# Four depthwise filters in one TensorE step: from 128x32 tiles, one filter at a time, to sixteen 32x32 tiles

## The reference, cut to what matters

```python
def _causal_dw_conv(x_bcl, w_ck):          # one filter for each channel, no sum over channels
    K = w_ck.shape[-1]
    return lax.conv_general_dilated(x_bcl, w_ck[:, None, :], window_strides=(1,),
                                    padding=[(K - 1, 0)], feature_group_count=x_bcl.shape[1])
```

## Time and profile before

| what | us |
|---|---|
| median of three runs (1008.17, 1003.43, 1007.61) | 1007.61 |
| span of the profiled execution | 1004.1 |
| TensorE busy | 932.3 (93%) |
| VectorE busy | 742.6 (74%) |
| ScalarE busy | 650.3 (65%) |
| GpSimd busy | 334.5 (33%) |

### The profile page before, as it was taken

The page is one execution under the profiler, slowest core; times in us unless marked ns, Lnnn a source line. Parts: engine busy times, 40 slices in busy tenths (PEclk is TensorE's granted clock), DMA queues, the critical chain, the costliest instruction groups (busy, mean ns, idle before and its releaser), DMA issues.

```text
span 1004.1 us, 22014 instructions
## 1 busy us (share of the span) xinstructions
PE 932.3 (93%) x7958; PEld 593.9 (59%) x7958; DVE 742.6 (74%) x2882; ACT 650.3 (65%) x1474; POOL 334.5 (33%) x720
## 2 busy tenths in 40 slices
...
GB/s 308 175 2 1 1 1 52 2 83 14 95 128 75 43 70 17 44 22 12 1 12 1 11 11 1 53 60 94 90 97 76 57 21 22 2 11 1 12 1 32
DMA packets 77692, 45.44 MB, mean 45 GB/s; under 512 B 53008, under 2 KB 68880, under 8 KB 77328
## 3 DMA queue, kind: packets, MB, share of 16 engines
...
## 4 chain that ended last, share of the span: by engine, by line
PE 57%; DVE 27%; ACT 8%; POOL 4%; issue 3%; DMA 0%; SPq 0%; POOLq 0%; ACTq 0%; DVEq 0%
PE psum L1101 7%; DVE pool L1588 5%; DVE sol_t L1593 5%; PE psum L558 5%; PE psum L1091 4%; PE psum L859 4%; PE psum L833 3%; PE psum L831 3%; PE psum L994 3%; DVE pool L1531 3%; PE psum L920 3%; PE psum L1085 2%; PE psum L1087 2%; ACT pool L1823 2%; PE psum L567 2%
## 5 line engine op out<-in xcount | busy, mean ns | idle before, releaser
L1809 ACT ACTIVATE pool<-psum 128x512 f32<-128x512 f32 x144 | 84.0, 595 | 64.4 <-PE psum L558 22.4
L2185 POOL TENSOR_SCALAR small<-small 128x4 f32<-128x4 f32 x88 | 22.2, 252 | 283.6 <-DVE small L1173 281.4
L1823 ACT ACTIVATE pool<-pool,small 128x128 f32<-128x128 f32 x224 | 91.5, 486 | 27.3 <-POOL small L2190 27.1
L558 PE MATMUL psum<-sb_const,pool 128*128 128x128 f32 x672 | 100.9, 283 | 6.4 <-ACT pool L1823 2.9
L920 PE MATMUL psum<-pool,firw 128*32 128x512 f32 (+7 forms) x960 | 103.2, 571 | 0.0
L558 PEld LDWEIGHTS psum<-sb_const,pool 128*128 128x128 f32 x672 | 79.3, 145 | 37.9 <-issue 22.3
L2188 POOL TENSOR_TENSOR small<-small,minus_half 128x4 f32<-128x4 f32 x88 | 92.2, 1048 | 7.3
L994 PE MATMUL psum<-pool,sb_l1a 128*128 128x512 f32 x192 | 88.6, 612 | 0.0
L1101 PEld LDWEIGHTS psum<-sb_l1f,pool 128*128 128x128 f32 x640 | 77.2, 192 | 11.3 <-issue 9.5
L1101 PE MATMUL psum<-sb_l1f,pool 128*128 128x128 f32 x640 | 82.8, 278 | 0.0
L1404 DVE TENSOR_TENSOR pool<-pool,psum 128x512 f32<-128x512 f32 x80 | 52.4, 682 | 37.8 <-ACT pool L2095 16.2
...
## 6 DMA issues: line engine op xcount, KB each, us to landing
...
```

The lines of the kernel that those rows point to most:

```text
L558: m = e.transpose(f.ap[:, part(b)], src[:, part(b)], ident)
L1809: e.activation(slot(g, i), f.ap, ACT.Copy).then_inc(f.emptied, 1)
L1823: m = e.activation(dst[:, part(b)], src[:, part(b)], ACT.Identity, bias=v["nm"][:, b:b + 1], scale=v["r"][:, b:b + 1])
```

## The change

- `vsh` is laid out otherwise: row `4u + s` of a block of 32 rows holds channel `u` (of eight) shifted by `s`. `b_sh` writes `v` with four DMAs in place of one and reads it back into every fourth row.
- `b_fir` is one step. For each of eight tap groups it issues sixteen matmuls of 32 rows and 32 columns: the 32 rows are eight channels by four shifts, the 32 columns are these eight channels for each of four filters. Four PSUM banks are filled at once. It stands where `b_fir.3` stood, and `b_fir.0` to `b_fir.2` are gone from the list.
- `b_ez` goes from GpSimd to VectorE, as one bitwise-and with a mask, and stands right before `b_fir` in the list.
- A new setup step `s_w` (16 matmuls and seven VectorE operations) brings the taps to their rows, and `s_b2` makes `firw` by a memset and 16 small products.
- The rows of `router_W1` are loaded in the new channel order (18 DMAs in place of one), and `b_lt`, `b_w`, `b_mx`, `b_ac` take the results in the new layout.

```diff
-c_ft/6 f_gl/2 b_q/1 b_vs/1 f_lg/3 c_fa/6 c_hF/7 b_fir.3/0 b_kk/0
+c_ft/6 f_gl/2 b_q/1 b_vs/1 f_lg/3 c_fa/6 c_hF/7 b_ez/0 b_fir/0 b_kk/0
...
-b_gg/1 b_ks/2 b_k2/2 b_fir.3/1 b_sh/2 b_x.38-40/0 f_e.2/3 b_ez/2 b_x.41-42/0 b_kk/1
+b_gg/1 b_ks/2 b_k2/2 b_ez/1 b_fir/1 b_sh/2 b_x.38-40/0 f_e.2/3 b_x.41-42/0 b_kk/1
...
+b_x.23-24/1 b_ez/2 b_fir/2 b_x.25/1 b_u.0/0 b_x.26-28/1 b_kk/2
+b_gg/3 b_x.32-34/2 b_ez/3 b_fir/3 b_kk/3
+b_gg/4 f_gw/7 b_q/5 b_k/5 g_out/2 b_q/6 b_ez/4 b_fir/4 f_e.0/7 b_kk/4
+b_x.42-44/4 b_q2/6 f_na/7 b_ez/5 b_fir/5 b_kk/5
+b_x.8-20/5 b_ez/6 b_fir/6 b_rs/4 b_xt/4 b_x.21/5 b_rl/4 b_u.0/4 b_x.22/5 b_sh/7 b_kk/6
+b_x.18-31/6 b_ez/7 b_fir/7 b_xt/5 b_p.2/4 b_x.32/6 b_kk/7
...
         def b_sh(g, k):                                    # SyncE
-            e.dma_start(kept, slot(g, 5)).then_inc(sem(f"v_out{a}"), 16)
+            for r in range(4):
+                e.dma_start(by_row[r], slot(g, 5)[32 * r:32 * r + 32]).then_inc(sem(f"v_out{a}"), 16)
...
-                e.dma_start(vsh[32 * s:32 * s + 32, :, s:],
-                            kept.rearrange("(c p) m -> p c m", c=4)[:, :, 0:GT - s]).then_inc(sem(f"shifted{a}"), 16)
+                e.dma_start(vsh[s:P:4, :, s:],
+                            kept.rearrange("(u c) m -> u c m", c=4)[:, :, 0:GT - s]).then_inc(sem(f"shifted{a}"), 16)
...
         def b_fir(g, k):                                   # TensorE
-            o.wait_ge(sem("edge_zeroed"), 3 * g + 3)
+            o.wait_ge(sem("edge_zeroed"), g + 1)
+            heads_f = [begin("b_fir", g, f"h{r}") for r in range(4)]
-            for n, kg in enumerate(kgs):
-                for c in range(4):
-                    col = FIR_GROUPS.index((k, kg)) * 4 + c
-                    m = e.matmul(b4(f.ap)[32 * c:32 * c + 32, :, 4 * kg:], firw[:, col, :],
-                                 vsh[:, c, :, 0:P - 4 * kg], start=n == 0, stop=n == len(kgs) - 1)
+            for kg in range(NKG):
+                for r in range(4):
+                    r_ = slice(32 * r, 32 * r + 32)
+                    for c in range(4):
+                        m = e.matmul(b4(heads_f[r].ap)[32 * c:32 * c + 32, :, 4 * kg:], firw[r_, kg, c, :],
+                                     vsh[r_, c, :, 0:P - 4 * kg], start=kg == 0, stop=kg == NKG - 1)
+                    if kg == NKG - 1:
+                        m.then_inc(heads_f[r].filled, 1)
...
+        def b_ez(g, k):                                    # VectorE
+            cells = slot(g, 8, 4).bitcast(mybir.dt.int32).rearrange("p (q t) -> p q t", t=P)[:, :, 0:3]
+            o.wait_ge(sem(f"shifted{g % NA}"), 64 * (g // NA + 1))
+            o.settle()
+            e.tensor_tensor(cells, cells, edge[:, :].unsqueeze(1).to_broadcast([P, NP, 3]), ALU.bitwise_and).then_inc(
+                sem("edge_zeroed"), 1)
...
         def b_fir(g, k):                                   # ScalarE
-            evacuate("b_fir", g, 3 + k, k)
+            for r in range(4):
+                f = full("b_fir", g, f"h{r}")
+                e.activation(slot(g, 3 + r), f.ap, ACT.Copy).then_inc(f.emptied, 1)
...
         def b_w(g, k):                                     # VectorE
-            e.tensor_tensor(w3, w3, rep(mq, 5), ALU.mult).then_inc(*o.link())
+            e.tensor_tensor(flat(v["spread"]).rearrange("p (q c f) -> p q c f", c=4, f=4), w3[:, :, 0:4].unsqueeze(2).to_broadcast(shp),
+                            mq.unsqueeze(2).unsqueeze(3).to_broadcast(shp), ALU.mult).then_inc(*o.link())
+            e.tensor_tensor(v["ms"], mq, w3[:, :, 4], ALU.mult).then_inc(*o.link())
...
-        def b_ez(g, k):                                    # GpSimd
-            for s in range(1, 4):
-                settle()
-                e.memset(vsh[32 * s:32 * s + 32, :, :, 0:s], 0.0).then_inc(*mark("edge_zeroed", 3 * g + s))
```

More of the change, by code:

```diff
@@ L51 @@
[L51 to L85, removed]
@@ L101 @@
-f_e.4-5/7 b_qs/5 b_q2/5 b_v/6 f_d.0-2/7 b_vs/6 f_d.3/7 b_ks/6 f_d.4/7 b_ez/5 f_d.5/7 f_out/7 b_x.0-3/4 b_ss/5
-b_fir.0/5 b_x.4-5/4 b_k2/6 b_qs/6 b_x.6-7/4 b_sh/6 b_ez/6 b_qn/5 b_x.8-9/4 g_na/3 g_out/3 b_x.10-31/4 b_gg/5
-b_x.32-41/4 b_vT/5 b_x.42-44/4 b_fir.1/5 b_q2/6 f_na/7 b_fir.2-3/5 b_kk/5 b_fir.0/6 b_x.45-52/4 b_ag/5 b_x.53-58/4
-b_vT/6 b_x.59/4 b_ss/6 b_x.60-61/4 b_xo/4 b_tr/7 b_q/7 b_k/7 b_qs/7 b_v/7 b_vs/7 b_sol/5 b_x.0-1/5 b_qn/6 b_x.2-3/5
-b_gg/6 b_x.4-6/5 b_ks/7 b_k2/7 b_fir.1/6 b_x.7/5 b_fir.2/6 b_x.8-20/5 b_fir.3/6 b_rs/4 b_xt/4 b_x.21/5 b_rl/4 b_u.0/4
@@ new lines @@
+f_hid.1/3 f_e.2-3/2 f_hid.2/3 b_sh/1 c_ft/7 f_e.4-5/2 b_qs/1 b_ag/0 b_sol/0 b_x.0-4/0 b_ks/1 b_x.5-6/0 c_nb/6 f_d.0-1/2
+b_x.7/0 f_d.2-4/2 b_q2/1 f_mu/3 b_k2/1 f_d.5/2 b_ss/1 b_x.8/0 f_out/2 b_x.9/0 f_cnt/3 b_x.10/0 c_fa/7 f_gl/3 b_vT/1
+b_x.11/0 b_x.12-13/0 b_qn/1 b_x.14-18/0 f_hid.3-4/3 f_na/2 b_x.19-30/0 f_gw/3 b_tr/2 b_v/2 b_x.31/0 c_park/6 b_x.32-35/0
+f_hid.5/3 b_x.36-37/0 b_k/2 b_vs/2 f_e.0-1/3 b_gg/1 b_ks/2 b_k2/2 b_ez/1 b_fir/1 b_sh/2 b_x.38-40/0 f_e.2/3 b_x.41-42/0
+b_kk/1 b_ag/1 f_d.0-1/3 f_e.3-4/3 c_nb/7 f_e.5/3 b_x.43-46/0 b_q/2 b_x.47/0 b_qs/2 b_q2/2 b_x.48-49/0 f_d.2-4/3
```

253 lines of the change are left out of this document (168 added, 85 removed).

## The result

The changed kernel takes 1103.4 us (median of four runs, 1099.2 to 1105.2) against 1005.5 for the kernel before (median of four, 1001.1 to 1008.2): a ratio of 1.097, 95% interval 1.093 to 1.101. The profiled execution has a span of 1101.7 us (before 1004.1) and a mean granted TensorE clock of 0.909 (before 0.959). Forecast were 1080 and 1037 to 1118: the direction and the mechanism are right, and the size is 23 us short.

The account below looks back on a forecast made before the run. VectorE was taken as the bound in the two filter stages. 51.2 (wait) + 22.4 (clock) + 2.6 (ScalarE) + 2.6 (setup) + 1.5 (`b_w`) - 6.7 - 1.0 = 72.6 us more, forecast 1080 us, range 1037 to 1118.

Parts of the forecast that it names:

- The wait that comes in: At `b_fir` in all eight groups: TensorE waits for `b_ez`, then VectorE stops for the filter step; 51.2 us in sum.
- TensorE's lead there: Group 6: TensorE read as starting the filters at 717.55, 15 us before VectorE reaches that place.
- both engines are 6.1 us earlier here for the waves that went: Group 4: removed waves were in the chain, so the new wait costs only 0.7 us there.
- the 1.0 for group 0: Group 0: a gain of 1.0 us for the piece like group 4's removed waves.
- The tile step: Each sixteen-tile `b_fir` step: taken to last 6.26 us like `b_fir.3`, upper end 7.9 by weight loads.
- rival 3: Filter steps: sixteen tiles don't overlap fully; 7.9 us a step gives 1093, other cases 1105 or 1130; chance 15%.
- The clock: Eight filter steps: TensorE runs at a lower clock after idling, 2.8 us each, 22.4 us in all.
- VectorE's own waits: In the two stages with filters: VectorE's existing waits of 6.7 us give way, subtracted in full.
- The setup: At the start: VectorE's added operations in `s_w` and `s_b2` cost 2.6 us, between 0 and 5.7.
- ScalarE's bunch: Behind the filters in groups 0 and 4: four bunched copies make TensorE wait 1.3 us each, 2.6 in all.
- The second: Behind the filter steps: other engines use the pause and the clock stays up; 1040 us, chance 13%.
- the first: Whole kernel: TensorE was the bound and gets its time back; 1004.6, or 959 if all busy time counted; chance 4%.

Follow-up runs that it names:

- experiment 1: Changed kernel with the eight `b_ez` words 5 to 17 us earlier in the list, so the mask precedes TensorE's need: 1021.5 us, ratio 1.018.
- experiment 2: Kernel before, plus an unused VectorE addition right before each group's `b_fir.3`, which waits for it: 1080.3 us, ratio 1.076.
- Experiment 8: Kernel before with `b_fir.0` to `b_fir.2` cut to four matmuls of 32x8 columns each, `b_fir.3` whole: 1009.7 us, ratio 1.005.
- 3: Kernel of experiment 1 with the two inner loops of `b_fir` swapped, so neighbouring matmuls lie in different row blocks: 1025.5 us, ratio 1.022.
- 4: Changed kernel with unread matmuls of 128x384 columns filling TensorE's idle time before each `b_fir` wait: 1090.6 us, ratio 1.085.
- 5: Kernel of experiment 1 with `b_fir`'s matmuls over two of the four sequences, half the token columns: 1024.0 us in one run.
- 6: Kernel of experiment 1 with `b_fir` loops reordered so only eight of sixteen tiles can work at a time: 1068.5 us in one run.
- 7: Kernel of experiment 1 with the whole `b_fir` step moved earlier into TensorE's idle gaps in groups 0 to 4 and 7: 1026.6 us, ratio 1.023.
- 9: Kernel of experiment 1 with `b_fir` in halves, tap groups 0 to 3 earlier, 4 to 7 at the old place: 1035.5 us, ratio 1.031.
- 10: Kernel of experiment 1 with unread matmuls of 128x384 columns in seven idle gaps of TensorE: 1017.8 us, ratio 1.011.
- experiment 11: Kernel before with the change's setup added: `s_w`, memset and 16 products of `s_b2`, 18 DMAs; the old product stays: 1012.7 us, ratio 1.008.
- 12: Kernel before with `b_fir.3` lengthened from eight to ten waves, without a wait on VectorE: 1007.2 us, ratio 1.003.

## Why the prediction was right, and where its size was off

- **The wait that comes in** is shown from both sides: taken out it gives 8% back (1), put into the old kernel it costs 7.6% (2). The stall and the 2.8 us of clock predicted for each group against experiment 2, which has the step length assumed: group 0 11.4 against 10.6, 1 8.1 and 9.3, 2 9.6 and 8.1, 3 10.7 and 10.3, 5 10.7 and 10.2, 6 9.6 and 9.4, 7 10.0 and 9.6. Group 4 was 3.5; without the 6.1 us for the waves, which experiment 2 keeps, that is 9.6, against 9.3. All eight places of experiment 2 grow by 76.8 us, of which 20.7 are the clock; the other 56.1 stand against a predicted 51.2 + 6.1 = 57.3. One reading was off: the row at 717.55 has 112 records, and the 64 of `b_fir.3/6` begin at 722.54, so TensorE's lead there was some 10 us and not 15. The stall was not worked out from it.
- **The step that failed: "both engines are 6.1 us earlier here for the waves that went"** (group 4, 0.7 us), and with it the 1.0 for group 0. The waves were in the chain, yet behind them stood another wait, for ScalarE. TensorE comes earlier only to stand 3.17 us idle and then runs slower. VectorE's lag shows both halves: it falls from 49.6 to 45.8 us at 719.60, and stands at 60.7 behind the filters. Experiment 8 measured the saving by itself: the lag falls from 1.6 to -2.2 us and is 3.1 behind the filters, and the whole is below nothing, +5 us. The prediction asked what is late next everywhere but here.
- **The tile step** was taken as 6.26 us, with the weight loads' 7.9 as the upper end and as rival 3. It is 7.93 to 7.95 at full clock (experiments 1, 3 and 4), 8 x 1.69 = 13.5 us: the upper end was right, but by luck. The 31 ns to a weight load that gave it are 23 in the changed kernel (46.6 us for 2048), the loads are busy 4.95 of 7.90 us of a step in experiment 1 (207.6 to 215.5 us), and half the columns (5) or fewer tiles in flight (6) move the step while the loads stay. What holds it at 7.95 is open. So the filters' busy time fell by 22.7 us in the changed kernel (40 at full clock), not by 53. The Trainium skill ("TensorE: Matmul & The Clock Gate", part 3) would have had an estimated 9.4 by its 10.6 times; the measurement decides, and it lies between 6.26 and 9.4.
- **The clock**, 22.4 us: the eight steps take 80.5 us where 8 x 7.95 are 63.6, so 16.9 are in the steps; filling the idle time gave back 12 (4). Right in kind, a little too large.
- **VectorE's own waits**, 6.7 us subtracted in full, did not give way: the lag falls by no more than 0.3 us between 315 and 671 us, and the steps of the staircase are whole. That was wrong.
- **The setup**, 2.6 us: 2.4 by the lag there, 1.0 to 2.6 in the traces of experiments 1, 3 to 7, 9 and 10 with the same setup, and up to 6 by experiment 11. Of the rest of the start's 4.9 us, the profiled run had lost 1.4 before the setup, which may be chance, and loses 1.3 between 191 and 200 us, where the small waves of group 0 stood: the 1.0 us of gain there is a loss (0.8 in experiment 8, none in 2, 11 and 12, which keep the waves).
- **ScalarE's bunch**, 2.6 us: `b_kk` waits for its banks 1.30 us in group 1 and 0.25 to 0.33 in three others, about 2.

With the measured sizes: 51.2 + 6.1 (group 4) + 13.5 + 16.9 + 4.9 + 2.6 (`b_w` and the end) + 2 = 97.2 us, against the span's 97.6; the single terms are not known that well, so that it closes this nearly is in part chance. Of the rivals, the third is right in its size, 7.9 us a step, as a term beside the main one, and not in its cause, the weight loads. The second is out: nothing came back behind a step. So is the first.

Of what is left in experiment 1 (18 us) the pieces measured alone are 5 for the lost small waves (8), 1 to 6 for the setup (1.0 by the lag there in experiment 1, up to 6 by experiment 11), 4 for the step's length (12) and 1 to 3 for the end, 11 to 18 in all. That they are independent is argued, not shown. Nor do they name the place where the trace of experiment 1 grows most: 5.9 us in group 1, where VectorE waits 6.0 us for `f_e`; why is open. No version beat the kernel before.
